# Two pre-norm transformer layers with a routed mixture of experts: gate weights that travel with the routed row, normalisation moved to ScalarE, and one step of a DMA queue reordered

## The chip, the cores and the metric

One core of a Trainium2 chip. The metric is device time in microseconds of one execution of the whole program; the runs of the kernel before are three.

## The reference, cut to what matters

The input is 8 sequences of 1024 tokens, 256 wide, float32. Four sub-layers follow, each with a residual and a layer norm in front: windowed attention with projection, a mixture of experts, block-sparse attention, a ternary linear layer. The change touches the parts around the mixture of experts:

```
logits = xf @ gate_w.T                       # 8 experts
topk_logits, topk_idx = top_k(logits, 2)
topk_w = softmax(topk_logits)                # = 0.5 +- 0.5*tanh((l1 - l2)/2)
for e in range(8):
    y = (silu(xf @ wg[e].T) * (xf @ wu[e].T)) @ w_down[e].T      # 384 hidden
    out = out + comb[:, e:e+1] * y
x = x + out + shared(xf)                     # one shared expert for every token
x = x + attention(layernorm(x))              # starts with q, k, v projections
```

## The kernel before, in words

The kernel is a row of stages with a barrier between two; each names its tiles with a prefix. Every engine has its program written out in order, and waits on semaphores; nothing is scheduled by a planner. The tokens stay in SBUF as `x_res`, 64 tiles of 128 tokens. A chunk is 4 tiles (512 tokens), 16 chunks in all. Products are done in three float16 terms from high and low parts (`split3`, lines 83 to 85).

`stage_project` (prefix `p`, runs twice: `p0` before the first attention, `p1` before the second). For each chunk: statistics of the rows (`bn_stats`, `bn_aggr`, VectorE lines 329, 332), square root on ScalarE (`root`, 407), reciprocal and normalisation on VectorE (`norm`, 337 and 343, four instructions of 128x256), transposes on TensorE (451), high part on ScalarE (`high`, 414), low part on VectorE (`low`, 352), 48 matmuls for q, k and v, then ScalarE writes q and k twice (`queries_keys`, 422 and 426, eight instructions), GpSimd subtracts to get their low parts (397), VectorE writes v (`values`, 361). Loads and stores are on SyncE's queue. In `p1` the statistics are preceded by merging: the two routed results of a token are loaded from DRAM (`yb`) and VectorE adds each with its gate weight to `x_res` (323, eight instructions of 128x256 a chunk).

`stage_route` (prefix `g`), a loop over the 16 chunks `s`. ScalarE normalises the rows of chunk `s+2` and writes their high part into `xrow` (`row_hi`, 1274 and 1280), VectorE writes the low part (`row_lo`, 1323), SyncE turns the rows with four DMA transposes (`turn`, 1197) into `xt`, TensorE makes the gate logits (`gates`), VectorE finds the top two (`top2`, 1330 to 1354) and the row number of each token in its experts' lists (`slots`, 1359 to 1368), GpSimd sends the rows there by indirect DMA into the DRAM table `xs` (1242, eight a chunk). Beside that the shared expert is computed in two halves of a chunk (`up`, `down` on TensorE; `silu` and `high` on ScalarE; `hidden`, part of the low parts and `add_y` on VectorE; `low` on GpSimd, 1250). And the weights of all experts, 27 parts, are brought in through a buffer of two (`w32`): SyncE loads (`load`, 1183), ScalarE makes the high part (`weight_hi`, 1267), VectorE the low part (`weight_lo`, 1318). Three parts come ahead of the loop, two in each of chunks 0 to 11 (`weight_parts`). The order of SyncE's queue in a chunk is: turn chunk `s+2` (waits until `row_lo` has written it), load the two weight parts, store a finished chunk of `x_res`. ScalarE's order in a chunk is: first half of the shared expert, `row_hi(s+2)`, first weight part, second half, second weight part. A difference of the two top logits per token is kept, and at the end of the stage one Tanh (1312) and two VectorE instructions (1450, 1451) make the gate weights.

`stage_routed` (prefix `e`): 71 tiles `j` of 256 rows of `xs`, each of one expert. SyncE transposes the rows in and loads two words of each row, token and expert (`col`, 1602); VectorE works out from them where each result goes (`address`, 1675 to 1685, five small instructions); TensorE does the expert's products (54 matmuls), ScalarE empties the result with one plain copy (`copy_y`, 1657, 128x512), GpSimd scatters the rows to `y2` (1630). At tile 4 four DMAs bring the gate weights into the order of tiles that the second layer uses (`swap_halves`).

Of the kernel before, what the change touches and what calls it, by code (L numbers as in the profile page):

```python
# [219 lines left out]
def stage_project(nc, tag, x_res, ident, w_in, b_in, qx, kx, vx, x_dram=None, y2=None, gate_w=None):  # L220
# [3 lines left out]
    with ExitStack() as ctx:  # L224
# [11 lines left out]
        std, rstd = sb("std", [P, 2, TC], F32), sb("rstd", [P, 2, TC], F32)  # L236
# [12 lines left out]
        rooted, inverted, normed = sem("rooted"), sem("inverted"), sem("normed")  # L249
# [8 lines left out]
        def _(sp):  # L258
# [52 lines left out]
        def _(dve):  # L311
            due = [0] * NC

            def statistics(c):
                k, r = c % 2, c % YR if merging else c
                due[r] += 16 * ((6 if c % 2 == 0 else 2) if merging else 1)
                dve.wait_ge(loaded[r], ONE + due[r])
                for n in range(2 if merging else 0):
                    if n:
                        dve.wait_ge(merged, ONE + 2 * TC * c + TC)  # L320
                    for t in range(TC):
                        ti = c * TC + t
                        dve.scalar_tensor_tensor(out=x_res[:, ti, :], in0=yb[:, r, n, t, :],
                                                 scalar=gate_w[:, ti, n:n + 1], in1=x_res[:, ti, :],
                                                 op0=ALU.mult, op1=ALU.add).then_inc(merged, 1)
                if merging:
                    dve.wait_ge(merged, ONE + 2 * TC * (c + 1))
# [41 lines left out]
            norm(0)  # L369
# [7 lines left out]
            norm(1)  # L377
            statistics(2)
            dve.wait_ge(s_set, ONE + 2)
            for c in range(NC):  # L380
                if c + 1 < NC:
                    low(c + 1)
                if c + 2 < NC:
                    norm(c + 2)
# [16 lines left out]
        def _(act):  # L401
# [6 lines left out]

            def high(c):
# [6 lines left out]
            def queries_keys(c):  # L416
# [3 lines left out]
                for m in range(4):  # L420
                    act.wait_ge(qk_ready, ONE + 4 * c + m + 1)
# [9 lines left out]
            root(1)  # L431
            act.wait_ge(s_w, ONE + 64)
            for j in range(3):
                act.activation(wh[:, j], w32[:, j], ACT.Copy, scale=WS).then_inc(s_wh, 1)
            high(0)
# [631 lines left out]
def swap_halves(eng, dst, src, sem):  # L1067


    d, s = (a.rearrange("p (b t) w -> p b t w", t=TB) for a in (dst, src))  # L1070
    eng.dma_start(d[0:64, :, 0, :], s[0:64, :, 0, :]).then_inc(sem, 16)
    eng.dma_start(d[64:P, :, 0, :], s[64:P, :, TB - 1, :]).then_inc(sem, 16)
    eng.dma_start(d[0:64, :, 1:TB, :], s[64:P, :, 0:TB - 1, :]).then_inc(sem, 16)
    eng.dma_start(d[64:P, :, 1:TB, :], s[0:64, :, 1:TB, :]).then_inc(sem, 16)


# [17 lines left out]
class Routing:  # L1094


    def __init__(self, sb, w_turned):
# [4 lines left out]
        self.w, self.w_turned = sb("moe_w", [P, NT, 2], F32), w_turned  # L1102


def stage_route(nc, tag, x_res, mean, rstd, ident, gate_in, up_in, down_in, ew, rt, xs, x_dram):


    with ExitStack() as ctx:
        def sb(n, shape, dt):
# [12 lines left out]
        xrow = sb("xrow", [P, XR, TC, 2 * D + 4], F16)  # L1122
# [8 lines left out]
        dif, th = sb("dif", [P, NT], F32), sb("th", [P, NT], F32)  # L1131
# [10 lines left out]
        zeros = spare[:, 1500:1500 + 2 * (D + 2)].rearrange("p (t w) -> p t w", t=2)  # L1142
# [23 lines left out]
        x_stored, counted, dif_done, th_done, table, pads, padded = (sem(n) for n in (  # L1166
            "x_stored", "counted", "dif_done", "th_done", "table", "pads", "padded"))
# [9 lines left out]
        def _(sp):  # L1177
# [45 lines left out]
        def _(pool):  # L1223
# [40 lines left out]
        def _(act):  # L1264
# [16 lines left out]

            def silu(s, h, f):
# [28 lines left out]
            act.wait_ge(dif_done, ONE + 1)  # L1311
            act.activation(th[:, :], dif[:, :], ACT.Tanh, scale=0.5).then_inc(th_done, 1)

        @block.vector
        def _(dve):
# [11 lines left out]
            def top2(c):  # L1327
# [3 lines left out]
                dve.wait_ge(routed, b + 1)  # L1331
                for t in range(TC):
# [631 lines left out]
```

## Time and profile before

| | us |
|---|---|
| median of three runs | 3210.08 (3198.16 to 3218.04) |
| the profiled execution | 3220.43 |
| its span, first to last instruction | 3218.7 |
| mean granted TensorE clock, share of full | 0.832 |

The profiled execution is one run with the hardware profiler; its rows say what each engine did and when, in us from the start of the span. A row of the timeline gives start, duration, engine, line, operation, output<-inputs, count, and in brackets the engine's idle time before it with what ended it; "x4" is four such instructions in a row, with their duration together. Stages by time: `p0` from 9 to 170, `g` from 1175 to 1545, `e` from 1549 to 1988, `p1` from 1996 to 2208; attention and the rest fill what lies between and after.

### The profile page before, as it was taken

The page shows a single profiled execution, that of the slowest core. Times are in us where ns is not written, and L with a number is a line of the kernel's source. Part 1 is how long each engine was busy: PE and PEld are TensorE (multiplying, and loading weights), DVE is VectorE, ACT ScalarE, POOL GpSimd, SP SyncE. Part 2 cuts the span into 40 slices and gives each one's busy share as a digit, 9 for nine tenths or more (in the row PEclk, how much of TensorE's full clock was granted, in tenths as well). Part 3 has the DMA queues.
Part 4 walks back from the last instruction along what each step waited for, and adds up shares of the span by engine and source line. Part 5 has one row for each costly group of instructions (what it writes and reads, how often), then busy time and mean ns, then how long its engine had stood idle before and what let it go on. Part 6 is the DMA issues. An engine that isn't in the chain of part 4 may idle for free. (4 is left out here: it accounts for less than half of the span.)

```text
span 3218.7 us, 81517 instructions
## 1 busy us (share of the span) xinstructions
PE 2391.7 (74%) x25933; PEld 1381.7 (43%) x25933; DVE 2043.7 (63%) x5809; ACT 1565.5 (49%) x3598; POOL 984.4 (31%) x1271
## 2 busy tenths in 40 slices
PE   7917888888856645668799996783588888888336
PEld 4602222222215534556688885441133333333225
DVE  7827777777715544445444443991789888887278
ACT  5605666666650023334244442551278777778202
POOL 3503433434434014556466664341000000000005
PEclk9957877878876667778899998896699999999658
DMA  6521222222201114444555344563022222221123
GB/s 205 201 87 32 63 64 68 64 62 69 68 29 55 42 49 118 115 122 138 118 130 145 90 90 101 189 230 113 21 68 65 62 65 62 63 67 46 52 72 104
DMA packets 361817, 290.14 MB, mean 90 GB/s; under 512 B 226304, under 2 KB 294656, under 8 KB 361408
## 3 DMA queue, kind: packets, MB, share of 16 engines
q1 hardware_dynamic: 348448, 249.32, 27.2%
q0 software_dynamic: 12960, 35.54, 3.4%
q8 instruction: 235, 3.85, 0.5%
q14 instruction: 174, 1.43, 0.1%
HBM read 133.46 MB, written 123.62 MB: 80 GB/s over the span
## 5 line engine op out<-in xcount | busy, mean ns | idle before, releaser
L766 ACT ACTIVATE a_pr<-a_pst 128x384 f32<-128x384 f32 (+3 forms) x2176 | 935.9, 483 | 398.7 <-PE a_pst L790 360.7
L714 DVE TENSOR_REDUCE a_mx<-a_psc 128x1 f32<-128x384 f32 (+2 forms) x1152 | 592.2, 567 | 140.1 <-PE a_psc L790 130.3
L709 DVE CUSTOM_DVE_ANT_0 a_cut<-a_psc,row_mask 128x384 bf16<-128x384 f32 (+1 forms) x1024 | 499.7, 522 | 209.1 <-PE a_psc L790 174.6
L857 PE MATMUL a_po<-a_pr,a_ve 128*17 128x128 f32 (+3 forms) x10496 | 622.8, 328 | 1.6 <-ACT a_pr L766 1.0
L790 PE MATMUL a_psc<-a_ke,a_qe 52*128 52x128 f16 (+5 forms) x3072 | 411.8, 312 | 249.5 <-DMA a_ke<-mrow 114.5
L790 PE MATMUL a_pst<-a_qe,a_ke 53*128 53x128 f16 (+5 forms) x3072 | 399.4, 303 | 104.4 <-ACT a_pr L766 44.3
L688 POOL TENSOR_SCALAR_AFFINE_SELECT a_pr<-a_pr 128x512 f32<-128x512 f32 x448 | 275.0, 634 | 496.2 <-ACT a_pr L766 496.2
L1796 POOL TENSOR_TENSOR x_res<-x_res,t_bias 128x256 f32 (+1 forms) x64 | 44.5, 726 | 967.4 <-DVE t_xn L185 967.4
L790 PEld LDWEIGHTS a_pst<-a_qe,a_ke 53*128 53x128 f16 (+1 forms) x3072 | 122.6, 95 | 468.3 <-ACT a_pr L766 234.3
L790 PEld LDWEIGHTS a_psc<-a_ke,a_qe 52*128 52x128 f16 (+1 forms) x3072 | 130.0, 97 | 407.1 <-issue 160.2
L857 PEld LDWEIGHTS a_po<-a_pr,a_ve 128*17 128x17 f32 x10496 | 198.3, 98 | 239.0 <-issue 154.8
L1691 DVE SCALAR_TENSOR_TENSOR e_hid<-e_pgu,e_gate 128x256 f32<-128x256 f32 x213 | 90.4, 425 | 247.1 <-ACT e_gate L1646 247.1
L83 PE MATMUL e_pgu<-e_xt,uh 128*128 128x256 f16 x852 | 233.5, 274 | 14.2 <-DMA e_xt<-xs 14.2
L84 PE MATMUL e_pgu<-e_xt,uh 128*128 128x256 f16 x852 | 233.5, 274 | 0.0
L85 PE MATMUL e_pgu<-e_xt,ul 128*128 128x256 f16 x852 | 233.4, 274 | 0.0
L397 POOL TENSOR_TENSOR p_stg<-p_qk,p_stg 128x512 f16<-128x512 f32 x128 | 148.8, 1176 | 223.8 <-ACT p_qk L426 222.1
L1646 ACT ACTIVATE e_gate<-e_pgu 128x256 f32<-128x256 f32 x213 | 81.0, 381 | 244.7 <-PE e_pgu L85 244.7
L83 PE MATMUL g_pgu<-g_xt,uh 128*128 128x256 f16 x384 | 118.8, 309 | 103.6 <-DVE g_hid L1375 103.6
L957 PE MATMUL c_ptok<-ident,c_ot 68*128 68x68 f32 x512 | 73.0, 307 | 153.9 <-DMA c_ot<-ox 110.8
L1622 POOL TENSOR_TENSOR e_hl<-e_hid,e_hh 128x256 f16<-128x256 f32 x213 | 141.2, 675 | 130.6 <-ACT e_hh L1650 129.1
L1242 POOL DMA_INDIRECT xs<-g_xrow,g_slot x128 | 126.8, 991 | 83.6 <-DVE g_slot L1368 51.3
L1630 POOL DMA_INDIRECT y<-e_yst,e_dest x142 | 138.1, 973 | 37.0 <-issue 34.4
(217 smaller groups left out, 4324.0 us busy)
## 6 DMA issues: line engine op xcount, KB each, us to landing
a_qe<-qx SPq DMA_DIRECT2D x384, 64.0 KB, 2.6
a_ke<-kx SPq DMA_DIRECT2D x384, 64.0 KB, 2.6
vx<-p_vst SPq DMA_DIRECT2D x32, 544.0 KB, 3.1
a_ve<-vx SPq DMA_DIRECT2D x64, 272.0 KB, 3.2
ox<-a_ost SPq DMA_DIRECT2D x256, 68.0 KB
c_ot<-ox SPq DMA_DIRECT2D x32, 544.0 KB
qx<-p_stg SPq DMA_DIRECT2D x64, 256.0 KB, 3.3
kx<-p_stg SPq DMA_DIRECT2D x64, 256.0 KB, 3.1
```

The source lines that it names most:

```text
L83: pe.matmul(out, stat_hi(p), mov_hi(p), start=(a == 0), stop=False)
L84: pe.matmul(out, stat_hi(p), mov_lo(p), start=False, stop=False)
L85: last = pe.matmul(out, stat_lo(p), mov_hi(p), start=False, stop=(a == n - 1))
L397: pool.tensor_tensor(stg[:, b % 2, m, 1, cols], qk32[:, m, :], stg[:, b % 2, m, 0, cols], ALU.subtract).then_inc(qk_lo, 1)
L688: pool.affine_select(out=edge, in_=edge, compare_op=ALU.is_ge, fill=0.0, base=0, pattern=[[0, 4], [sign, width]], channel_multiplier=-sign)\
L709: dve.tensor_tensor_reduce(out=cut[:, n % 4, 0:width], in0=psc[n % RING][:, 0:width], in1=row_mask[:, at:at + width], scale=1.0, scalar=-3 ...
L714: dve.tensor_reduce(out.unsqueeze(1), psc[n % RING][:, 0:width], AXX, ALU.max)\
L766: act.activation(pr[s % SLOTS][:, h // 2, h % 2, 0:width], pst[k % RING][:, 0:width], ACT.Exp, scale=scale).then_inc(p_ready, 1)
L790: last = pe.matmul(outs[par][:, col:col + count], stats[par], movs[par](tok, count), start=(k == 0), stop=(k == len(pieces) - 1), skip_gro ...
L857: last = pe.matmul(po[h][32 * a:32 * a + VW, tok % CH:tok % CH + w], ve[g][:, t, a * VW:(a + 1) * VW], pr[s % SLOTS][:, a // 2, a % 2, col ...
L1622: pool.tensor_tensor(hl[:, j % 2, f, :], hid[:, f, :], hh[:, j % 2, f, :], ALU.subtract)\
L1630: pool.indirect_dma_start(y2[:, :], bass.IndirectOffsetOnAxis(ap=dest[:, g, t:t + 1], axis=0), yst[:, g, t, :], None).then_inc(scattered[g ...
```

## The change

It does five things. (1) In `stage_project`, the normalisation of a row goes from VectorE to ScalarE: VectorE computes reciprocal and `shift` = -mean*reciprocal (`invert`), ScalarE applies both in four instructions, put between the second and third output of `queries_keys`. (2) The merge in `p1` becomes two plain additions of 128x1024. (3) In `stage_route`, SyncE loads the weight parts of a chunk ahead of turning chunk `s+2`, and ahead of the loop it loads part 2 before turning chunk 0. (4) The Tanh of a chunk's logit difference is taken in that chunk (`weigh`), written into the row, which grows from 516 to 518 float16 values and is sent as 32-bit words. (5) In `stage_routed`, `address` has three more small instructions that turn that value into the gate weight of the row (`share`), `copy_y` is two instructions of 128x256 with that weight as scale and waits for `address`; `swap_halves` and the gate weights at the end of `stage_route` go.

```diff
@@ stage_project, SyncE and VectorE
-                    sp.wait_ge(merged, ONE + 2 * TC * (c - YR + 1))
+                    sp.wait_ge(merged, ONE + 2 * (c - YR + 1))
...
-                        dve.wait_ge(merged, ONE + 2 * TC * c + TC)
-                    for t in range(TC):
-                        ti = c * TC + t
-                        dve.scalar_tensor_tensor(out=x_res[:, ti, :], in0=yb[:, r, n, t, :],
-                                                 scalar=gate_w[:, ti, n:n + 1], in1=x_res[:, ti, :],
-                                                 op0=ALU.mult, op1=ALU.add).then_inc(merged, 1)
+                        dve.wait_ge(merged, ONE + 2 * c + 1)
+                    dve.tensor_tensor(xc, xc, yb[:, r, n, :, :], ALU.add).then_inc(merged, 1)
...
-            def norm(c):
+            def invert(c):
                 k = c % 2
                 dve.wait_ge(rooted, ONE + c + 1)
+                if c >= 2:
+                    dve.wait_ge(normed, ONE + TC * (c - 1))
                 dve.reciprocal(rstd[:, k, :], std[:, k, :]).then_inc(inverted, 1)
                 dve.wait_ge(inverted, ONE + c + 1)
                 dve.wait_ge(gathered, ONE + TC * (c + 1))
-                if c >= 2:
-                    dve.wait_ge(turned, ONE + EC * (c - 1))
-                for t in range(TC):
-                    dve.tensor_scalar(xn[:, k, t, :], x_res[:, c * TC + t, :], mv[:, k, t, 0:1], rstd[:, k, t:t + 1],
-                                      ALU.subtract, ALU.mult).then_inc(normed, 1)
+                dve.scalar_tensor_tensor(out=shift[:, k, :], in0=mv[:, k, :, 0], scalar=-1.0, in1=rstd[:, k, :],
+                                         op0=ALU.mult, op1=ALU.mult).then_inc(shifted, 1)
@@ stage_project, ScalarE
+            def norm(c):
+                k = c % 2
+                if c >= 2:
+                    act.wait_ge(turned, ONE + EC * (c - 1))
+                act.wait_ge(shifted, ONE + c + 1)
+                for t in range(TC):
+                    act.activation(xn[:, k, t, :], x_res[:, c * TC + t, :], ACT.Identity, bias=shift[:, k, t:t + 1],
+                                   scale=rstd[:, k, t:t + 1]).then_inc(normed, 1)
...
                 for m in range(4):
+                    if m == 2 and c + 2 < NC:
+                        norm(c + 2)
@@ stage_route, SyncE
+            load(2)
             turn(0)
-            load(2)
             turn(1)
             for s in range(NC + 2):
+                for n in weight_parts(s):
+                    load(n)
                 if s + 2 < NC:
                     turn(s + 2)
-                for n in weight_parts(s):
-                    load(n)
@@ stage_route, GpSimd
-                            xs[:, :], bass.IndirectOffsetOnAxis(ap=slot[:, c * TC + t, n:n + 1], axis=0),
-                            xrow[:, c % XR, t, :], None).then_inc(scattered[c % XR], 16)
+                            xs[:, :].bitcast(U32), bass.IndirectOffsetOnAxis(ap=slot[:, c * TC + t, n:n + 1], axis=0),
+                            xrow[:, c % XR, t, :].bitcast(U32), None).then_inc(scattered[c % XR], 16)
...
+                pool.wait_ge(weighed, ONE + s + 1)
@@ stage_route, ScalarE
+            def weigh(c):
+                act.wait_ge(routed, ONE + c * RT + 10)
+                act.activation(xrow[:, c % XR, :, 2 * D + 4:2 * D + 6].bitcast(F32), dif[:, c % 2, :].unsqueeze(2),
+                               ACT.Tanh, scale=0.5).then_inc(weighed, 1)
...
+            weigh(0)
             for s in range(NC):
                 for h in range(2):
                     silu(s, h, 0)
                     silu(s, h, 1)
+                    if h and s + 1 < NC:
+                        weigh(s + 1)
                     high(s, h, 0)
...
-            act.wait_ge(dif_done, ONE + 1)
-            act.activation(th[:, :], dif[:, :], ACT.Tanh, scale=0.5).then_inc(th_done, 1)
@@ stage_routed
                 sp.dma_start(col[:, j % GR, :, :],
-                             xs[bass.ds(row, SL), 2 * D:2 * D + 4].bitcast(U32).rearrange("(t p) w -> p t w", p=P))\
+                             xs[bass.ds(row, SL), 2 * D:2 * D + 6].bitcast(U32).rearrange("(t p) w -> p t w", p=P))\
...
-                if j == GR:
-                    swap_halves(sp, rt.w_turned[:, :, :], rt.w[:, :, :], w_moved)
...
-                act.activation(yst[:, g, :, :], py[j % 2][:, :, :], ACT.Copy).then_inc(y_copied, 1)
+                act.wait_ge(addressed, ONE + AD * (j + 1))
+                for t in range(2):
+                    act.activation(yst[:, g, t, :], py[j % 2][:, t, :], ACT.Copy, scale=share[:, j % 2, t:t + 1])\
+                       .then_inc(y_copied, 1)
...
+                dve.tensor_scalar(sign[:, k, :], second[:, k, :], -YS / T, 0.5 * YS, ALU.mult, ALU.add)\
+                   .then_inc(addressed, 1)
...
+                dve.tensor_tensor(part[:, k, :], sign[:, k, :], col[:, g, :, 2].bitcast(F32), ALU.mult)\
+                   .then_inc(addressed, 1)
+                dve.wait_ge(addressed, b + 7)
+                if j >= 2:
+                    dve.wait_ge(y_copied, ONE + 2 * (j - 1))
+                dve.tensor_scalar(share[:, k, :], part[:, k, :], 0.5 * YS, None, ALU.add).then_inc(addressed, 1)
```

## Rows read from the trace of the kernel before

**Rows 1.** Stretches: busy us of PE, PEld, DVE, ACT, POOL, then clock, DMA share, GB/s.

```profile
40.00:160.00 120.00, 120.00 (x775) 76.84 (x774) 105.90 (x214) 82.78 (x151) 65.17 (x56) 1.00 0.51 188
1190.00:1486.00 296.00, 187.88 (x1712) 154.81 (x1713) 131.33 (x486) 109.44 (x238) 147.60 (x147) 0.79 0.43 116
1486.00:1525.00 39.00, 37.43 (x382) 32.32 (x381) 26.91 (x107) 17.46 (x44) 32.19 (x36) 1.00 0.52 158
1600.00:1900.00 300.00, 300.00 (x2750) 268.21 (x2748) 129.25 (x408) 129.78 (x356) 200.73 (x255) 1.00 0.51 119
2031.00:2181.00 150.00, 123.99 (x729) 74.83 (x728) 148.17 (x325) 78.34 (x143) 60.26 (x53) 0.94 0.62 210
```

**Rows 2.** Waits of stage g, 1175 to 1545: total us, times, longest.

```profile
ACT uh L1267 <- DMA g_w<-up_w: 90.0, 8, 12.7
...
ACT dh L1267 <- DMA g_w<-down_w: 49.1, 5, 11.8
```

**Rows 3.** Timeline of SyncE's queue in stage g.

```profile
1179.75 5.26 SPq L1197 DMA_TRANSPOSE g_xt<-g_xrow  x4
...
1345.08 5.25 SPq L1197 DMA_TRANSPOSE g_xt<-g_xrow  x4
1350.37 1.08 SPq L1183 DMA_DIRECT2D g_w<-up_w  x2
```

**Rows 4.** Timeline of ScalarE in stage g.

```profile
1202.57 1.06 ACT L1280 ACTIVATE g_xrow<-g_xn 128x1024 f16<-128x1024 f32 x1
...
1354.98 0.84 ACT L1267 ACTIVATE uh<-g_w 128x768 f16<-128x768 f32 x1 [11.19 <-DMA g_w<-up_w]
...
1484.55 2.06 ACT L1274 ACTIVATE g_xn<-x_res,g_shift,rstd 128x256 f32<-128x256 f32 x4
1486.72 1.06 ACT L1280 ACTIVATE g_xrow<-g_xn 128x1024 f16<-128x1024 f32 x1
...
1500.35 1.06 ACT L1280 ACTIVATE g_xrow<-g_xn 128x1024 f16<-128x1024 f32 x1
```

**Rows 5.** Timeline of VectorE in stage g.

```profile
1190.28 0.18 DVE L1330 TENSOR_SCALAR g_logit<-g_small 128x32 f32<-128x32 f32 x1
...
1343.82 1.22 DVE L1323 SCALAR_TENSOR_TENSOR g_xrow<-g_xn,g_xrow 128x1024 f16<-128x1024 f32 x1 [1.47 <-ACT g_xrow L1280]
...
1479.85 0.99 DVE L1318 SCALAR_TENSOR_TENSOR dl<-g_w,dh 128x768 f16<-128x768 f32 x1 [0.35 <-ACT dh L1267]
...
1487.81 1.64 DVE L1323 SCALAR_TENSOR_TENSOR g_xrow<-g_xn,g_xrow 128x1024 f16<-128x1024 f32 x1 [1.47 <-ACT g_xrow L1280]
```

**Rows 6.** Timeline of GpSimd in two chunks without weights.

```profile
1496.59 0.99 POOL L1242 DMA_INDIRECT xs<-g_xrow,g_slot  x1 [0.31 <-DVE g_slot L1368]
...
1510.31 0.98 POOL L1242 DMA_INDIRECT xs<-g_xrow,g_slot  x1 [0.31 <-DVE g_slot L1368]
```

**Rows 7.** Timeline of VectorE through one chunk of p1.

```profile
2107.87 3.90 DVE L343 TENSOR_SCALAR p_xn<-x_res,p_mv,p_rstd 128x256 f32<-128x256 f32 x4
2111.69 1.27 DVE L361 SCALAR_TENSOR_TENSOR p_vst<-p_pv,p_bv 128x512 f32<-128x512 f32 x2
2112.89 3.36 DVE L323 SCALAR_TENSOR_TENSOR x_res<-p_yb,moe_wt,x_res 128x256 f32<-128x256 f32 x8
...
2118.03 1.26 DVE L352 SCALAR_TENSOR_TENSOR p_xl<-p_pt,p_xh 128x512 f16<-128x512 f32 x2
...
2119.40 3.97 DVE L343 TENSOR_SCALAR p_xn<-x_res,p_mv,p_rstd 128x256 f32<-128x256 f32 x4
```

**Rows 8.** Single lines: duration ns, minimum/median/maximum, first and last start.

```profile
L343 DVE TENSOR_SCALAR p_xn<-x_res,p_mv,p_rstd x128: 402/1240/1320, 16.5 to 2179.9; 128x256 f32<-128x256 f32 x128
...
L1058 DVE TENSOR_TENSOR x_res<-x_res,c_att x16: 1206/1215/1217, 3036.6 to 3126.5; 128x1024 f32 x14, 128x1024 f32<-128x1024 f32 x2
```

**Rows 9.** Tanh after Silu, and the one table load for Silu.

```profile
L1312 ACT ACTIVATE g_th<-g_dif x1: 238/238/238, 1539.1 to 1539.1; 128x64 f32<-128x64 f32 x1
...
L1285 ACT ACT_TABLE_LOAD x1 | 1.3, 1283 | 0.0
```

More of the change, by code:

```diff
@@ L217, in split_ready, with stage_project @@
             eng.wait_ge(self.lo_done[e], ONE + c + 1)
[L220 removed]
+def stage_project(nc, tag, x_res, ident, w_in, b_in, qx, kx, vx, x_dram=None, y2=None):
     merging = y2 is not None
@@ L235, in stage_project @@
         st, mv = sb("st", [P, 2, TC, 6], F32), sb("mv", [P, 2, TC, 2], F32)
-        std, rstd = sb("std", [P, 2, TC], F32), sb("rstd", [P, 2, TC], F32)
+        std, rstd, shift = (sb(n, [P, 2, TC], F32) for n in ("std", "rstd", "shift"))
         xn = sb("xn", [P, 2, TC, D], F32)
@@ L315, in statistics @@
                 k, r = c % 2, c % YR if merging else c
+                xc = x_res[:, c * TC:(c + 1) * TC, :]
                 due[r] += 16 * ((6 if c % 2 == 0 else 2) if merging else 1)
@@ L368, in _ @@
             statistics(1)
-            norm(0)
+            invert(0)
+            invert(1)
             dve.wait_ge(s_w, ONE + 64)
@@ L376, in _ @@
             low(0)
-            norm(1)
             statistics(2)
@@ L383, in _ @@
                 if c + 2 < NC:
-                    norm(c + 2)
+                    invert(c + 2)
                 values(c)
@@ L431, in _ @@
             root(1)
+            norm(0)
             act.wait_ge(s_w, ONE + 64)
@@ L434, in _ @@
                 act.activation(wh[:, j], w32[:, j], ACT.Copy, scale=WS).then_inc(s_wh, 1)
+            norm(1)
             high(0)
@@ L1064, in _ @@
             stats.finish(dve)
[L1067 to L1074, printed above, removed]
 class ExpertWeights:
@@ L1094, with __init__ @@
 class Routing:
-    def __init__(self, sb, w_turned):
+    def __init__(self, sb):
         self.expert, self.row = sb("tab_expert", [P, NJ], U32), sb("tab_row", [P, NJ], U32)
@@ L1121, in stage_route @@
         xn = sb("xn", [P, TC, D], F32)
-        xrow = sb("xrow", [P, XR, TC, 2 * D + 4], F16)
+        xrow = sb("xrow", [P, XR, TC, 2 * D + 6], F16)
         xt = sb("xt", [P, XR, 2 * EC, CH], F16)
@@ L1130, in stage_route @@
         slotf, slot = sb("slotf", [P, 2, TC, 2], F32), sb("slot", [P, NT, 2], U32)
-        dif, th = sb("dif", [P, NT], F32), sb("th", [P, NT], F32)
+        dif = sb("dif", [P, 2, TC], F32)
         gate, hid = sb("gate", [P, FC, SL], F32), sb("hid", [P, FC, SL], F32)
@@ L1141, in stage_route @@
         gone = [spare[:, 256 + n * NJ * E:256 + (n + 1) * NJ * E].rearrange("p (j e) -> p j e", e=E) for n in range(2)]
-        zeros = spare[:, 1500:1500 + 2 * (D + 2)].rearrange("p (t w) -> p t w", t=2)
+        zeros = spare[:, 1500:1500 + 2 * (D + 3)].rearrange("p (t w) -> p t w", t=2)
         tj = [sb(f"tj{n}", [P, NJ], F32) for n in range(6)]
@@ L1165, in stage_route @@
         y_ready, y_added = [sem(f"y_ready{h}") for h in range(2)], [sem(f"y_added{h}") for h in range(2)]
-        x_stored, counted, dif_done, th_done, table, pads, padded = (sem(n) for n in (
-            "x_stored", "counted", "dif_done", "th_done", "table", "pads", "padded"))
+        x_stored, counted, weighed, table, pads, padded = (sem(n) for n in (
+            "x_stored", "counted", "weighed", "table", "pads", "padded"))
         RT = 21
@@ L1331, in top2 @@
                 dve.wait_ge(routed, b + 1)
+                if c >= 2:
+                    dve.wait_ge(weighed, ONE + c - 1)
                 for t in range(TC):
@@ L1446, in table_of_tiles @@
                    .then_inc(table, 1)
-            def gate_weights():
-                dve.wait_ge(th_done, ONE + 1)
-                dve.tensor_scalar(rt.w[:, :, 0], th[:, :], 0.5 * YS, 0.5 * YS, ALU.mult, ALU.add).then_inc(table, 1)
-                dve.tensor_scalar(rt.w[:, :, 1], th[:, :], -0.5 * YS, 0.5 * YS, ALU.mult, ALU.add).then_inc(table, 1)
-                dve.wait_ge(table, ONE + 26)
             dve.scalar_tensor_tensor(out=shift[:, :], in0=mean[:, :], scalar=-1.0, in1=rstd[:, :],
@@ L1483, in _ @@
                 add_y(s, 0)
-                if s + 2 == NC:
-                    dve.wait_ge(routed, ONE + (s + 1) * RT + 17)
-                    dve.sem_inc(dif_done, 1)
             add_y(NC - 1, 1)
-            gate_weights()
+            dve.wait_ge(table, ONE + 24)
         @block.tensor
@@ L1567, in stage_routed @@
         xt = sb("xt", [P, GX, 2 * EC, SL], F16)
-        col = sb("col", [P, GR, 2, 2], U32)
+        col = sb("col", [P, GR, 2, 3], U32)
         gate, hid = sb("gate", [P, FC, SL], F32), sb("hid", [P, FC, SL], F32)
@@ L1575, in stage_routed @@
         dest = sb("dest", [P, GR, 2], U32)
+        sign, part, share = (sb(n, [P, 2, 2], F32) for n in ("sign", "part", "share"))
         pgu = [ctx.enter_context(nc.psum_tensor(f"{tag}_pgu{f}", [P, 2, SL], F32)) for f in range(FC)]
@@ L1587, in stage_routed @@
         scattered = [sem.from_zero(f"scattered{g}") for g in range(GR)]
-        w_moved, x_loaded = sem("w_moved"), sem("x_loaded")
-        AD = 5
+        x_loaded = sem("x_loaded")
+        AD = 8
         sem.start()
@@ L1626, in scatter @@
                 g = j % GR
-                pool.wait_ge(y_copied, ONE + j + 1)
+                pool.wait_ge(y_copied, ONE + 2 * (j + 1))
                 pool.wait_ge(addressed, ONE + AD * (j + 1))
@@ L1674, in address @@
                 dve.wait_ge(loaded[g], ONE + 16 * (j // GR + 1))
-                dve.tensor_copy(colf[:, k, :, :], col[:, g, :, :]).then_inc(addressed, 1)
+                dve.tensor_copy(colf[:, k, :, :], col[:, g, :, 0:2]).then_inc(addressed, 1)
                 dve.wait_ge(addressed, b + 1)
@@ L1720, in down @@
                 if j >= 2:
-                    pe.wait_ge(y_copied, ONE + j - 1)
+                    pe.wait_ge(y_copied, ONE + 2 * (j - 1))
                 for f in range(FC):
```

17 lines of the change are left out of this document (7 added, 10 removed).

## The prediction

> **What bounds the kernel now.** I read the table of stretches first, since the change touches three stages with different limits [rows 1]. In `p0` (40 to 160) TensorE is busy 120.00 of 120 us at full clock: 775 matmuls, 56 to a chunk, so 8.67 us a chunk, and nothing on another engine shows. In `e` (1600 to 1900) it is 300.00 of 300 us. In `p1` (2031 to 2181) VectorE has 148.17 of 150 us and TensorE waits. In `g` (1190 to 1486) no engine is full: TensorE 188, GpSimd 148 of 296 us, clock 0.79. Such a stretch is waiting for something outside the engines, and the list of waits says what: ScalarE waited 90.0 + 49.1 us in 13 pieces for weight parts to land [rows 2]. The timeline shows why. `turn` of the next chunk is ahead of the loads on SyncE's queue; its four transposes take 5.25 us to issue, from 1345.08, the loads follow at 1350.37, and ScalarE gets the first at 1354.98 after 11.19 us idle [rows 3, 4]. ScalarE is in order, so the second half of the shared expert stands behind that wait. The second part of `row_hi` starts at 1202.57 in turn 0 of the loop and at 1486.72 in turn 12, 23.7 us a turn; from turn 12 to 13, which have no weights, the step is 13.63 us [rows 4].
>
> **Part 3, the loads ahead of `turn`.** The loads of a chunk now stand before a wait on `row_lo(s+2)` and behind one on the buffer, which the previous chunk's `weight_lo` frees. After that VectorE still does a low part, `add_y`, `slots` and three products, and ScalarE a `row_hi` of 2.06 + 1.06 us, before the part is wanted. I put that at 8 us after the first buffer is free, from the order of the program and the chunk of 13.63 us. A load took 1354.98 - 1350.37 = 4.6 us behind four transposes. So it is hidden with about 3 us to spare, and the 11 us stall goes. `turn` is pushed back only by the issue of two loads, 1.08 us, and its rows are wanted a chunk later.
>
> What is late next is what bounds a chunk without weights. GpSimd repeats there in 1510.31 - 1496.59 = 13.72 us with 0.31 us idle at that point, waiting for `slots` [rows 6]. A second ring has the same length: `row_hi`, `row_lo`, `top2`, `hidden`, `slots`, `hidden`, `high`, `row_hi`, 13.63 us between ScalarE and VectorE [rows 4]. Two `weight_lo` of 0.93 to 0.99 us lie on that ring, with 0.35 us for the second `weight_hi` [rows 5], less about 0.5 us of waiting that they fill: 13.63 + 1.75 = 15.4 us, and 0.1 for the chunk's Tanh and contention, 15.5. Bounds: 14.0 if the ring absorbs most of it, 17.5 if the loads land later in a denser queue. Twelve periods go from (1486.72 - 1202.57)/12 = 23.7 us to 15.5: 98 us, bounds 74 and 116. The DMA share, 0.43 at 23.7 us a chunk, becomes 0.66 at 15.5.
>
> Ahead of the loop the order costs. `turn(0)` started at 1179.75 and now waits for load 2, which waits for the first `weight_lo`; that puts it near 1185.7. But the first `top2` began only at 1190.28, behind the third `weight_lo` [rows 3, 5], so not all 6 us reach it. I take 3, bounds 0 and 6.
>
> **Part 4.** `weigh` is one instruction of 128x4 per chunk, under the 238 ns of the 128x64 one [rows 9], and its input is ready before the `hidden` that ScalarE waits for anyway. GpSimd's new wait on it was met a chunk ahead. The Tanh before came after Silu with no table load of its own; the stage has the one load of 1283 ns [rows 9]. I take no switch inside the loop, and at most one more load ahead of it, beside TensorE's first products. The one Tanh and two small instructions at the end save under 0.5 us.
> The Trainium skill ("ScalarE: Activation LUTs", section Table sets: the hidden batching unit) says that functions of different sets cost a load at each change and should be batched by set; interleaving Tanh with Silu would then speak against this change. Taken so, it is the third rival below; the trace agrees that both are served by one set here.
>
> **Part 1 and 2, `p1`.** The four `norm` instructions took 3.90 us of an 11.53 us chunk [rows 7]. One such takes 402 ns at its shortest and 1240 in the median [rows 8]: it is slow when GpSimd's subtraction runs. It goes, against a reciprocal (as now) and a `shift` of 0.2 us. Merging took 3.36 us for eight; two additions of 1215 ns take 2.45 [rows 7, 8]. VectorE falls to 11.53 - 3.9 - 0.9 + 0.2 = 6.9 us a chunk, and TensorE's 8.67 would be next. ScalarE is busy 82.78 us over 13.84 chunks in `p0`, 5.98 each, and gets 2.06 more [rows 1, 4]: 8.0, still under 8.67. But a chain is longer: from the end of v's products, `values` (0.8 after it), merging 2.45, statistics 1.7, root and start 0.3, two pairs of outputs (four of the ten large instructions in ScalarE's 5.98 us, 0.57 each: 2.3), `norm` 2.06, and 0.1 of hand-overs give 9.6 us until the next transposes may start. Each chunk's rows are normalised two ahead, so two periods hold this chain and one TensorE chunk: (9.6 + 8.67)/2 = 9.1 us. GpSimd's subtractions now run while VectorE merges. In `g` an instruction with two SBUF inputs took 1.22 us, and 1.64 where it started beside a GpSimd subtraction [rows 5]; so I take 9.4, bounds 8.67 and 10.5. Over 13 chunks: 13 x (11.53 - 9.4) = 28 us, bounds 13 and 37.
> The Trainium skill ("SBUF — State Buffer", section SBUF: two separate sides) has the port pair of VectorE and GpSimd as an exclusive lock, also taken by a VectorE instruction with two SBUF inputs when GpSimd reads SBUF. By it the second addition would wait for one subtraction of 1.1 us (60.26 us over 53), and the chunk would be (9.6 + 1.1 + 8.67)/2 = 9.7 us, 24 us saved; the 1.64 beside 1.22 points the same way.
>
> `p0` has nothing to gain, being TensorE's. ScalarE's 8.0 us fits, and `norm` is done before the transposes need it. At its start and at that of `p1`, `norm(0)` and `norm(1)` stand with the weight parts on ScalarE, 2 us each, but the transposes of chunk 1 also wait for the low part of chunk 0: I take 0 in `p0` and -1 in `p1`, which merges faster, bounds -3 and +4 together.
>
> **Part 5, `e`.** TensorE is full, 5.9 us a tile (2750 matmuls in 300 us, 54 each) [rows 1]. ScalarE has 2.5 us a tile and gets under 0.3, VectorE 2.5 and at most 1.5, GpSimd the same work. The new wait of `copy_y` on `address` has the next tile's silus behind it on ScalarE; `address(j-1)` stands before `hidden(j)` on VectorE, so it is done when ScalarE comes to it. I take 0, bounds -1 and +5 (cover gone in a few tiles). The scatter of 32-bit words moves the same rows.
>
> **Sum.** -98 + 3 - 28 - 1 + 0 = -124 us. The profiled execution, 3220.4, would be 3096. It lies 10 us over the median of the runs, so against that median I say 3210 - 124 = 3086.
>
> **Rivals.**
> 1. The stall goes, but TensorE becomes the bound because its clock stays where it is. For: the clock of this stretch is 0.79 [rows 1], and a chunk needs about 13.1 us at full clock (37.43 of 39 us, at 13.7 us a chunk). Against: in 1486 to 1525 it is 1.00, with work not much denser than I expect. 13.1/0.79 = 16.6 us a chunk, 85 us saved in place of 98: 3099.
> 2. ScalarE bounds the projections. For: 8.0 us of work in 8.67 leaves 0.67 for its waits, and it now waits for statistics, for `shift` and for transposes in one order. Against: the norms stand where its inputs are old. If the waits take twice the spare time, `p0` loses 0.7 x 14 = 10 us: 3096.
> 3. Each Tanh switches tables twice: 32 loads of 1283 ns on the ring of ScalarE and VectorE, 41 us: 3127. Against: [rows 9].
> 4. Slower: the row pitch of `xs`, from 1032 to 1036 bytes, makes the transposing loads of `e` slow. They share a DMA load of 0.51 with the rest, 3.0 of 5.9 us a tile [rows 1]. To cost the 124 us that the rest gives, a tile must reach 7.65 us, so DMA work would have to grow 2.6 times, and from that point the whole is slower; at 3 times it is 9.0 us a tile, 71 x 3.1 = 220 us: 3306. Against: 1032 is no round pitch either.
>
> **How the numbers follow.** Forecast 0.73, first rival 0.12, second 0.07, third 0.05, fourth 0.02, the rest 0.01 for no change. The likeliest gives 3086. The best ends together (-116, -37, 0) give 3057, less the spread of the runs, 3050; the worst (-74 + 6 - 13) give 3129, which takes in rivals 1 to 3. About 1% (32 us) is what a measurement can tell from no change, with runs 20 us apart: faster 0.96, same 0.02, slower 0.02.
>
> **What would show it.** In the new profile of `g`: no wait of ScalarE for `g_w` over 2 us after the first, `row_hi` about every 15.5 us in chunks 1 to 12, clock near 1.00, the stage about 95 us shorter. In `p1`: transposes every 9.4 us, VectorE no longer full. In `p0` 8.67 us a chunk, in `e` 5.9 us a tile, and one table load in `g`, two at most. Wrong it would be if weights still stall ScalarE, if a tile of `e` grows, or if ACT_TABLE_LOAD appears per chunk.

## The result and the profile after

The changed kernel takes 3103.28 us (median of 4 runs, 3093.11 to 3108.87), the kernel before beside it 3214.06 (3198.16 to 3219.72): a ratio of 0.966, 95% interval 0.962 to 0.970. That is 111 us less, where 124 were forecast. The profiled execution took 3108.87 us, with a span of 3107.1, against 3220.43 and 3218.7.

Where the time went is read best from the stages. Each begins at the first instruction that only it has, in the two profiled executions:

| stage | before, us | after, us | difference | forecast |
|---|---|---|---|---|
| `p0` to the first scores | 216.6 | 216.3 | -0.3 | -1 with `p1`'s start |
| `a0`, `c0` (unchanged) | 958.4 | 958.1 | -0.3 | 0 |
| `g` | 385.2 | 292.6 | -92.6 | -95 |
| `e` | 435.9 | 433.0 | -2.9 | 0 |
| `p1` to the first scores | 265.1 | 250.5 | -14.6 | -28 |
| `a1`, `c1` and the rest (unchanged) | 957.5 | 956.6 | -0.9 | 0 |

The unchanged part agrees here by chance. Over the fourteen profiles of this study `a0`, `c0`, `a1` and `c1` together lie between 1828 and 1861 us, with no edit in them, while `g` comes within 1 to 3 us again in every kernel with the same `g`. So the stages below are compared by their own length, and totals that lie less than 15 us apart are not told apart. Two rows of the table need the same care. The changed `e` takes 433.0 to 433.8 us in most profiles and 436.2 to 436.3 in three (e3, e4, e6), the old one 435.5 and 435.9, so its -2.9 is no gain that is shown. The changed `p1` takes 248.2 to 248.8 us in the three other profiles with the same `p1` (e2, e8, e9), so the gain there is 14.6 to 17 us.

The table of stretches after, with a stretch of `p0`, `g`, `e` and `p1` in turn; busy us of PE, PEld, DVE, ACT and POOL, then granted clock, DMA share and GB/s:

```profile
40.00:160.00 120.00, 120.00 (x775) 76.87 (x774) 57.96 (x174) 106.59 (x203) 64.47 (x57) 1.00 0.51 188
1210.00:1400.00 190.00, 158.35 (x1652) 136.25 (x1653) 139.67 (x459) 104.84 (x242) 149.31 (x143) 0.99 0.63 174
1500.00:1800.00 300.00, 300.00 (x2750) 268.40 (x2748) 146.53 (x560) 147.61 (x407) 200.29 (x255) 1.00 0.50 120
1935.00:2070.00 135.00, 121.00 (x746) 74.70 (x743) 102.75 (x210) 102.12 (x195) 64.08 (x52) 0.96 0.71 233
```

Against [rows 1]: `p0` and `e` are TensorE's as before, to the matmul. In `g` the clock has gone from 0.79 to 0.99 and TensorE is busy 83% of the stretch, not 64%. In `p1` VectorE is no longer full (76%), and yet TensorE is not full either.

The waits of ScalarE in `g` after, against [rows 2]:

```profile
ACT g_hh L1294 <- DVE g_hid L1382: 74.0, 62, 8.9
ACT g_xrow L1283 <- DVE g_dif L1344: 29.3, 15, 4.1
...
ACT dh L1266 <- DMA g_w<-down_w: 3.8, 1, 3.8
```

139 us of waiting for weight parts have become 3.8, once, ahead of the loop. What is left is waiting for VectorE: 103.3 us in these two rows, where the same view of the kernel before has 30.4. It has grown, but by less than the wait that went.

ScalarE's timeline in `g`, against [rows 4]:

```profile
1187.54 0.84 ACT L1266 ACTIVATE dh<-g_w 128x768 f16<-128x768 f32 x1 [3.77 <-DMA g_w<-down_w]
1188.40 1.28 ACT L1283 ACT_TABLE_LOAD   x1
1193.75 0.21 ACT L1283 ACTIVATE g_xrow<-g_dif 128x4 f32<-128x4 f32 x1 [4.06 <-DVE g_dif L1344]
1193.97 1.28 ACT L1289 ACT_TABLE_LOAD   x1
...
1233.11 2.06 ACT L1273 ACTIVATE g_xn<-x_res,g_shift,rstd 128x256 f32<-128x256 f32 x4
1248.92 2.06 ACT L1273 ACTIVATE g_xn<-x_res,g_shift,rstd 128x256 f32<-128x256 f32 x4
...
1375.40 2.06 ACT L1273 ACTIVATE g_xn<-x_res,g_shift,rstd 128x256 f32<-128x256 f32 x4
```

`row_hi` comes every 15.8 us (1233.11 to 1375.40 in nine steps; 15.5 forecast, 23.7 before). The first Tanh and the first Silu load a table each, and no other load follows in the loop.

### The profile page after: what moved, and what is told of

Read it like the earlier page. It is cut to its first block and busy times, and to the rows that moved or that the text cites. A ratio compares the mean times of both kernels' runs of the same rounds, so it can differ in the third digit from the quotient of the medians.

```text
span 3107.1 us, 81888 instructions
## 1 busy us (share of the span) xinstructions
PE 2357.4 (76%) x25933; PEld 1358.1 (44%) x25933; DVE 1970.9 (63%) x5828; ACT 1649.8 (53%) x3813; POOL 991.8 (32%) x1271
## 5 line engine op out<-in xcount | busy, mean ns | idle before, releaser
L966 PEld LDWEIGHTS c_ptok<-ident,c_ot 68*128 68x128 f32 x512 | 57.8, 197 | 166.9 <-issue 82.5
```

## The experiments

Each kernel ran beside the kernel before, and the ratio is to that. "A chunk of p1" is the mean of the steps between the transposes of one chunk and the next, from the third chunk on (11.55 us before, 10.3 in the changed kernel). Where a count of matmuls is given, it is the time by that count (56 a chunk) in the stretch 1935 to 2070; a few records are missing from some traces, so it can come out up to 0.2 us off.

**e1: the order of the queue alone.** In the kernel before:

```diff
             for s in range(NC + 2):
+                for n in weight_parts(s):
+                    load(n)
                 if s + 2 < NC:
                     turn(s + 2)
-                for n in weight_parts(s):
-                    load(n)
```

> The kernel before with one edit of the change alone: in the loop of g's SyncE queue the weight loads stand ahead of turn. Nothing else is taken over, and the prologue is as before. Theory: the order of the queue is the whole gain of g, which the two traces put at 385.2 - 292.6 = 92.6 us; so 90 to 97 us off the kernel before, a row_hi every 15.5 to 15.8 us in place of 23.7, ScalarE's waits for weight parts gone, p0, p1 and e as before. Rival: the order alone leaves a wait that another part of the change removes (the one Tanh at the end, or the prologue's load), and less than 80 us come.

Measured: ratio 0.971 (0.967 to 0.976), 86 us; `g` 290.1 us, 95.1 less than before; `p1` 265.4 and `e` 435.5, as before. `row_hi` every 15.83 us, and of the waits for weight parts this is left:

```profile
ACT dh L1267 <- DMA g_w<-down_w: 4.0, 1, 4.0
```

The order of two statements is the whole gain of `g`. It is even 2.5 us shorter than the changed kernel's, which also has `load(2)` ahead of `turn(0)`: from the stage's first instruction to the loop's first `row_hi` it is 25.4 us before and 25.3 here and in e2, and 28.6 in the changed kernel. That is the "+3" of the forecast. The totals are 86 us apart and `g` 95, which the spread of the unchanged stages covers: in the profile of e1 they were 26 us longer.

**e2: the change without that order.** In the changed kernel the loop's loads stand behind `turn` again, and `load(2)` behind `turn(0)`.

> The changed kernel with the old order of g's SyncE queue, in the loop and ahead of it; all else of the change stays. Theory: g goes back to 385 us and a row_hi every 23.7 us, the time to 92 us above the changed kernel; what is left against the kernel before is p1's 15 us and e's 3, so 0.992 to 0.995 of it. Rival: the parts help each other, and it is more than 100 us above the changed kernel.

Measured: ratio 0.996 (0.993 to 0.999), 11 us less than before; `g` 387.3 us, and the old waits are back:

```profile
ACT uh L1266 <- DMA g_w<-up_w: 92.6, 8, 13.3
ACT dh L1266 <- DMA g_w<-down_w: 50.5, 5, 12.5
```

The parts add up: `g` is 2 us longer than before, within what it varies by, and the gain is `p1`'s (248.3 us here). The ratio lies just above the 0.992 to 0.995 that I expected. The weighing by Tanh in `g` costs nothing that shows.

**e3: `p1` without GpSimd's subtraction.** In the changed kernel (with the low part of the staging tile filled with zero once):

```diff
-                    pool.tensor_tensor(stg[:, b % 2, m, 1, cols], qk32[:, m, :], stg[:, b % 2, m, 0, cols],
-                                       ALU.subtract).then_inc(qk_lo, 1)
+                    w = 8 if merging else CH
+                    part = slice(cols.start, cols.start + w)
+                    pool.tensor_tensor(stg[:, b % 2, m, 1, part], qk32[:, m, 0:w], stg[:, b % 2, m, 0, part],
+                                       ALU.subtract).then_inc(qk_lo, 1)
```

> The changed kernel, but in p1 GpSimd's subtraction for the low parts of queries and keys covers 8 of 512 columns; the other columns are filled with zero once, so the low parts are left out. Theory: the subtractions beside VectorE's additions made these slow (1318 ns in the median, up to 2170, where 1200 was taken), and the chain from v's products to the next transposes by it longer than 9.6 us. Without them the additions take 1.2 us each and a chunk of p1 (9.6 + 8.67)/2 = 9.1 us in place of 10.3: 15 us less than the changed kernel. Rival: the chain is long for another reason (ScalarE's order, the hand-overs), and p1 stays at 10.0 to 10.3 us a chunk.

Measured: a chunk 9.23 us by the count (819 matmuls in 135 us) and 9.3 by the steps, where 9.1 was expected; `p1` 237.5 us, 13 less than in the changed kernel. The total, ratio 0.964 (0.960 to 0.968), doesn't show it: the unchanged stages were 19 us longer in that profile. The additions, first in the changed kernel, then here (busy us, mean ns of one):

```profile
L322 DVE TENSOR_TENSOR x_res<-x_res,p_yb 128x1024 f32<-128x1024 f32 x26 | 43.1, 1656 | 0.4
```

```profile
L322 DVE TENSOR_TENSOR x_res<-x_res,p_yb 128x1024 f32<-128x1024 f32 x26 | 31.7, 1220 | 0.4
```

1656 ns beside the subtractions, 1220 without: 3.3 us a chunk against 2.44. The theory holds, in the size too.

**e4: statistics ahead of the copies of v.** In the changed kernel:

```diff
-                values(c)
                 if c + 3 < NC:
                     statistics(c + 3)
+                values(c)
```

> The changed kernel, but in both projections VectorE does the statistics (and merging) of a chunk ahead of the copies of v, not behind them; the same instructions. Theory: the chain of p1 begins at the end of v's products only because the copies stand ahead of the merging. With it parted, VectorE's 6.9 to 8 us of work a chunk fit in TensorE's 8.67, and p1 goes from 10.3 to 8.7 - 9.1 us a chunk: 16 to 21 us less than the changed kernel. p0 stays. Rival: a chain that goes through ScalarE (outputs of queries and keys, norm) or VectorE's contended work is as long, and p1 stays at 9.8 or more.

Measured: `p1` 241.7 us, 9 less where 16 to 21 were expected, a chunk 9.8 us. It is neither the one nor the other. The chain is parted, and a new wait has come. ScalarE's outputs and the additions no longer show; VectorE waits for the rows of y:

```profile
DVE x_res L322 <- DMA p_yb<-y: 21.5, 4, 6.1
```

SyncE's queue and VectorE say why:

```profile
1966.58 2.96 SPq L288 DMA_DIRECT2D qx<-p_stg  x4
1969.58 3.00 SPq L288 DMA_DIRECT2D kx<-p_stg  x4
1972.62 1.30 SPq L270 DMA_DIRECT2D p_yb<-y  x1
...
1981.78 2.48 DVE L322 TENSOR_TENSOR x_res<-x_res,p_yb 128x1024 f32<-128x1024 f32 x2 [5.99 <-DMA p_yb<-y]
```

The loads are behind eight stores, which take 6 us to issue. Their buffer had been free for three chunks. The total, ratio 0.968 (0.963 to 0.972), can't be told from the changed kernel's.

**e5: plain additions, norm back on VectorE.** The changed kernel with `norm` and `invert` of the projections as they were before.

> The changed kernel with norm of both projections back on VectorE as before; merging stays two plain additions. VectorE is then the bound of p1 again. Theory: eight instructions of 3.36 us become two of 2.45, so a chunk of p1 goes from 11.5 (before) to 10.6 us. Rival: beside GpSimd's subtractions two long additions lose as much as they save (they took 2.6 to 4.0 us in the changed kernel), and a chunk stays at 11.2 or more. g and e as in the changed kernel; the whole 5 to 15 us above it.

**e6: norm on ScalarE, merging in eight as before.**

```diff
-                    dve.tensor_tensor(xc, xc, yb[:, r, n, :, :], ALU.add).then_inc(merged, 1)
+                    for t in range(TC):
+                        ti = c * TC + t
+                        dve.scalar_tensor_tensor(out=x_res[:, ti, :], in0=yb[:, r, n, t, :], scalar=one[:, 0:1],
+                                                 in1=x_res[:, ti, :], op0=ALU.mult, op1=ALU.add).then_inc(merged, 1)
```

> The changed kernel with the merging of p1 as before, eight scalar_tensor_tensor (with a scalar of one, since the rows are already weighted); norm stays on ScalarE. Theory: the chain from v's products through merging to the next transposes is 0.9 us longer than in the changed kernel, a chunk 10.3 + 0.45 = 10.7 us or a little more; the move of norm is then worth 0.8 us a chunk of the 1.25 that p1 gained. Rival: the eight short instructions fit better between GpSimd's subtractions, and a chunk is 10.3 or less, so that the plain additions brought nothing.

Measured: e5 has `p1` at 252.5 us (ratio 0.970, 0.966 to 0.973), e6 at 266.4 (ratio 0.971, 0.968 to 0.974); before it was 265.1 and after 250.5. So the plain additions bring 12.6 us alone, and the move of `norm` alone brings nothing; on top of the additions it brings another 2 to 4 us. Merging of e5, then of e6:

```profile
L322 DVE TENSOR_TENSOR x_res<-x_res,p_yb 128x1024 f32<-128x1024 f32 x26 | 31.6, 1217 | 0.5
```

```profile
L324 DVE SCALAR_TENSOR_TENSOR x_res<-p_yb,p_one,x_res 128x256 f32<-128x256 f32 x96 | 64.8, 736 | 0.4
```

By busy time a chunk, merging takes 2.43 us in e5 and 5.4 in e6 (64.8 in 12 chunks); before it took 3.33 (43.3 us in 13 chunks of the stretch 2031 to 2181), and in the changed kernel 3.3. `norm` on VectorE had stood in GpSimd's way (four instructions of 1.04 us where the shortest is 0.40 [rows 8]). Moved to ScalarE, it left its place to the merging, which then stood in it. My expectation for e5 was met (10.67 for 10.6 us a chunk, by steps of 10.63 to 10.70). That for e6 was too low: 11.5 for 10.7, since I had the chain longer by 0.9 us and it was longer by 5.4 - 3.3 = 2.1; the clock in its stretch was 0.90 besides, where the changed kernel has 0.96.

**e7: rows of y asked for two chunks earlier.** In e4:

```diff
-                if c + ahead < NC:
-                    load_y(c + ahead)
+                for n in range(c + ahead + (2 if c else 0), c + ahead + 3):
+                    if merging and n < NC:
+                        load_y(n)
```

> As e4_statistics_early, but on SyncE's queue of p1 the rows of chunk c + 6 are asked for where chunk c + 4 was, ahead of the stores of chunk c (the same four buffers). In e4 VectorE waited 21.5 us in four pieces for these rows, once per pair of chunks, behind the stores of queries and keys. Theory: the place in the queue is the cause; the waits go, and a chunk of p1 takes TensorE's 8.7 to 8.9 us in place of 9.6 to 9.7: 12 us less than e4. Rival: the DMA engines themselves are the bound (share 0.74), the waits come back elsewhere, and a chunk stays above 9.3.

**e12: the same loads in the changed kernel,** with the statistics left in their place.

> The changed kernel with only the rows of y asked for two chunks earlier in p1, and the statistics behind the copies of v as before. Theory: in the changed kernel VectorE did not wait for these rows (the chain from v's products was later than they), so the stage stays at 10.0 to 10.3 us a chunk, 250 us in all; the place of the statistics is what opens the gain, and the loads are the wait that follows. Rival: earlier loads alone shorten p1 by over 5 us.

Measured: e7 has `p1` at 227.2 us, 23 less than the changed kernel, and the transposes are 8.67 us apart, which is TensorE's own time. VectorE no longer waits for rows of y; these are the longest waits of VectorE and ScalarE in the stretch 1935 to 2040:

```profile
DVE p_xl L349 <- ACT p_xh L420: 6.0, 12, 0.5
ACT p_stg L430 <- PE p_pqk L85: 5.2, 12, 0.5
DVE p_vst L358 <- PE p_pv L85: 3.0, 12, 0.3
```

The additions are as slow as ever there (1658 ns), but nothing waits for them. In e12 `p1` stays at 248.8 us, as expected. Both edits are needed, in that order: the chain hid the late rows. The totals, 0.966 (0.962 to 0.969) and 0.966 (0.960 to 0.972), are covered by the spread of the attention stages.

**e8: slots early in `g`.** In the changed kernel:

```diff
             for s in range(NC):
-                slots(s)
...
                 hidden(s, 1)
+                if s + 1 < NC:
+                    slots(s + 1)
                 for n in weight_parts(s):
                     weight_lo(n)
```

(and `slots(0)` ahead of the loop).

> The changed kernel, but in g VectorE does slots(s + 1) right after hidden(s, 1), ahead of the two weight_lo, low and add_y, where it stood behind them. In the changed kernel GpSimd waits there up to 1.2 us a chunk; its own work is 8 scatters at 1.27 us and four subtractions of 1.1, 14.7 us. Theory: GpSimd is the bound of g now, a chunk goes from 15.8 to 14.7 us, and g from 292.6 to 280. Rival: the ring between ScalarE and VectorE with weight_lo on it is the bound, and the chunk stays at 15.6 or more.

Measured: ratio 0.963 (0.960 to 0.965); `g` 274.6 us, 18 less than the changed kernel, a chunk 14.34 where 14.7 was expected. The instructions are the same. `slots` now ends 3 us after the products that it waits for begin (`ranks`, on TensorE; 1293.4 and 1290.4), where it ended 6 us after (1294.4 and 1288.3). But GpSimd, which it releases, waits for it hardly less (0.8 us a chunk, 1.2 before). What has changed is how long GpSimd's subtractions take. The changed kernel, then e8, each from 1220 to 1380:

```profile
L1248 POOL TENSOR_TENSOR g_hl<-g_hid,g_hh 128x256 f16<-128x256 f32 x42 | 47.1, 1142 | 0.5
```

```profile
L1248 POOL TENSOR_TENSOR g_hl<-g_hid,g_hh 128x256 f16<-128x256 f32 x46 | 31.8, 710 | 4.0 <-ACT g_hh L1294 2.6
```

Four a chunk, each 0.43 us shorter, are 1.7 us; the chunk lost 1.47. In the changed kernel one pair runs from 1291.39 to 1293.58, beside VectorE's `weight_lo` and `low`; in e8 a pair runs from 1291.68 to 1292.98, beside a `hidden` that reads PSUM and the small instructions of `slots`. And TensorE waited for these low parts in the changed kernel (total us, times, longest, in the same stretch); in e8 it has no such wait:

```profile
PE g_py L83 <- POOL g_hl L1248: 26.8, 20, 1.6
```

So the order of VectorE's program made GpSimd's chunk shorter. Whether the shorter subtractions alone give the 1.47 us, or the earlier release as well, was not tried apart.

**e9 to e11.** The changed kernel again, then with the edits of e7 and e8 together, then with one more of GpSimd's subtractions on VectorE:

> The changed kernel once more, unaltered, beside the two below, as their measure: a ratio of 0.963 to 0.969 to the kernel before, p1 at 10.1 to 10.3 us a chunk and g at 292 us. What its unchanged attention stages differ by from the first profile (a0 755.9, a1 769.0 us) is the size of what no edit causes; by the runs so far, up to 15 us either way.

> The changed kernel with the three edits that shortened a stage: statistics ahead of the copies of v and rows of y asked for two chunks earlier (p1), slots right after the second half's products (g). Theory: they touch different stages and add up: p1 23 us and g 18 us less than the changed kernel, so 3062 to 3070 us where that has 3105, ratio 0.951 to 0.955. Rival: the shorter stages leave TensorE's clock lower in the attention stages that follow, or their spread eats it, and less than 25 us come.

> As e10_all_three, and in g VectorE does the low part of the second third of the hidden units too, which GpSimd had. GpSimd's chunk falls from about 14 to 12.5 us (two subtractions of 0.7 to 1.1 us fewer), VectorE's rises from 11.0 to 12 - 12.8. Theory: with slots early, GpSimd is the bound of g (14.34 us a chunk in e8), so a chunk goes to 13.3 - 13.7 us, TensorE's 13.1 at full clock being next, and g loses 8 to 12 us more. Rival: the ring between ScalarE and VectorE is as long as GpSimd's work, the subtractions lie on it, and g stays or grows.

| | median, us | ratio (interval) | `g` | `p1` | unchanged four |
|---|---|---|---|---|---|
| e9 | 3122.27 | 0.965 (0.960 to 0.969) | 295.2 | 248.5 | 1849.3 |
| e10 | 3079.77 | 0.952 (0.948 to 0.957) | 275.2 | 227.3 | 1844.0 |
| e11 | 3092.10 | 0.956 (0.953 to 0.960) | 277.5 | 227.8 | 1841.0 |

e10 is 42 us faster than the changed kernel in the same series, which is 20 in `g` and 21 in `p1`: the gains add up, and it beats both kernels. e11 misses: a chunk of `g` was expected at 13.3 to 13.7 us. GpSimd's subtractions of e11 and what it waited for:

```profile
L1249 POOL TENSOR_TENSOR g_hl<-g_hid,g_hh 128x256 f16<-128x256 f32 x22 | 16.5, 751 | 13.8 <-ACT g_hh L1295 13.6
```

Its work fell from 126.85 us (e8) to 111.29 in 160, and `row_hi` still came every 14.24 us. So GpSimd's work was not the bound of `g` after e8. TensorE is busy 147 of these 160 us; what holds the chunk at 14.2 to 14.3 us stays open.

## Why the prediction was right, and where it was off

**Part 3.** Right in mechanism and in size. The stall came from the order of the queue and went with it (e1, e2). The period was forecast at 15.5 and is 15.8 us, the start at +3 and is +3.2 (28.6 against 25.4). What holds a chunk once the stall is gone was named less well. The forecast had two rings of one length, GpSimd's with its wait for `slots` and one between ScalarE and VectorE, and laid the two `weight_lo` on the second only. In the changed kernel GpSimd stood idle for `slots` only 1.2 us of 15.8 and TensorE waited for it 26.8 us in 160 (the rows at e8), so GpSimd was probably on the path too, with subtractions that were longer beside `weight_lo`. The 15.5 is near 15.8, but these runs do not show that the ring which the forecast took is the one that sets it. The first rival falls: the clock rose to 0.99, in e1 too, where nothing but the order was changed.

**Part 4.** Two table loads ahead of the loop and none in it: the third rival falls. The Trainium skill ("ScalarE: Activation LUTs", section Table sets: the hidden batching unit) asks for batching only across sets. Here Tanh following Silu needs no load, while Silu following the first Tanh did: the order of the first two decides.

**Part 1 and 2.** Here the forecast was off: 28 us, and 14.6 came (up to 17 in the other profiles), within the bounds of 13 to 37 but near the lower one. Two terms of the step failed. (The chain's terms also add up to 9.7 us and not to 9.6, which is 0.05 us a chunk.) The first is the merging. The step had "two additions of 1215 ns", raised the chunk from 9.1 to 9.4 for contention, and so priced the merging at about 3.0 (a chain of 2 x 9.4 - 8.67 = 10.1 us). The pair of rows that this rested on, 1.22 us and 1.64 beside a subtraction [rows 5], does not part the two cases: the one of 1.22, at 1343.82, ran beside subtractions as well (a pair from 1343.21 to 1345.57). It is longer where it counts. One chain of the changed kernel, from v's products to the late transposes:

```profile
1997.29 0.69 DVE L357 SCALAR_TENSOR_TENSOR p_vst<-p_pv,p_bv 128x512 f32<-128x512 f32 x1 [0.55 <-PE p_pv L85]
1997.90 4.03 DVE L322 TENSOR_TENSOR x_res<-x_res,p_yb 128x1024 f32<-128x1024 f32 x2
2001.97 1.41 DVE L326 BATCH_NORM_STATS2 p_st<-x_res 128x6 f32<-128x256 f32 x4
2003.40 0.38 DVE L329 BATCH_NORM_AGGREGATE p_mv<-p_st 128x2 f32<-128x6 f32 x4
...
2003.82 0.30 ACT L403 ACTIVATE p_std<-p_mv,p_eps 128x4 f32<-128x4 f32 x1 [4.17 <-DVE p_mv L329]
2004.03 0.67 ACT L429 ACTIVATE p_stg<-p_pqk,p_bqk_s 128x512 f16<-128x512 f32 x1
...
2006.30 2.07 ACT L411 ACTIVATE p_xn<-x_res,p_shift,p_rstd 128x256 f32<-128x256 f32 x4
...
1997.60 3.25 POOL L393 TENSOR_TENSOR p_stg<-p_qk,p_stg 128x512 f16<-128x512 f32 x2 [1.91 <-ACT p_qk L433]
...
2008.43 1.09 PE L460 MATMUL p_pt<-ident,p_xn 128*128 128x128 f32 x8 [2.50 <-ACT p_xn L411]
```

The pieces are those of the forecast, in its order, and each has its size but one: two additions and two subtractions begin together and take 4.03 and 3.25 us, where they take 2.43 and 2.3 apart. From 1997.29 to 2008.43 are 11.1 us, against 9.6 forecast, and the additions have all of the difference (1.6 us). The other late chain, with additions of 3.28 us from 2019.65, is 10.4 us (2019.05 to 2029.43). The rule of the Trainium skill that I had weighed ("SBUF — State Buffer", section SBUF: two separate sides), an exclusive port pair, gave 9.7 us a chunk; the trace agrees in direction, with both engines' instructions longer, and the measured 10.3 is nearer to it than to my 9.4. e3, which removes the subtractions, is at 9.23, and the formula without contention gives 9.1.

The second is TensorE's clock. The formula put TensorE's chunk at 8.67 us after each late one. The transposes of the changed kernel:

```profile
1947.29 1.09 PE L460 MATMUL p_pt<-ident,p_xn 128*128 128x128 f32 x8 [1.75 <-ACT p_xn L411]
1956.02 1.04 PE L460 MATMUL p_pt<-ident,p_xn 128*128 128x128 f32 x8
1967.36 1.09 PE L460 MATMUL p_pt<-ident,p_xn 128*128 128x128 f32 x8 [2.50 <-ACT p_xn L411]
1977.78 1.04 PE L460 MATMUL p_pt<-ident,p_xn 128*128 128x128 f32 x8
1988.36 1.09 PE L460 MATMUL p_pt<-ident,p_xn 128*128 128x128 f32 x8 [1.75 <-ACT p_xn L411]
```

Four chunks are 8.73, 11.34, 10.42 and 10.58 us, 41.1 together or 10.3 each, and the pattern repeats. After a wait of 1.75 us the next chunk takes 8.73; after one of 2.50 it takes 10.42. The clock by stretches in such a chunk:

```profile
2008.00:2010.00 2.00, 1.57 (x11) 1.16 (x12) 1.96 (x2) 2.00 (x5) 0.39 (x1) 0.89 0.98 316
2010.00:2012.00 2.00, 2.00 (x6) 0.73 (x5) 1.94 (x9) 1.77 (x5) 2.00 (x2) 0.50 0.06 19
2012.00:2014.00 2.00, 2.00 (x8) 0.79 (x7) 1.26 (x4) 1.50 (x4) 0.65 (x2) 0.75 0.50 188
2014.00:2016.00 2.00, 2.00 (x11) 0.88 (x9) 0.00 (x0) 2.00 (x5) 1.45 (x2) 1.00 1.01 380
```

It fell to the lower level, 1.2 GHz, for a good 3 us after the wait of 2.50 us, and half of that time is the 1.7 us that the chunk took more. With that chunk at 8.73 us, as after the shorter wait, the mean would be 9.85. So the clock has 0.4 of the 0.9 us a chunk that the forecast missed; that share is read from the trace and was not tried by itself. It follows from the first: in e3, without the subtractions, TensorE's waits are 0.94 us and its clock is 1.00 in the same stretch.

What the forecast had not seen at all is what e5 and e6 show: relieving VectorE of `norm` was priced as 3.9 us a chunk off the engine that bounds, and is worth nothing alone and 2 to 4 us in all beside the additions. The engine was relieved (102.75 of 135 us, which is 7.8 a chunk where 6.9 was forecast), but the bound was already a chain through the copies of v, the merging and ScalarE, just as long. The forecast named this chain and took it for shorter than it was.

**Part 5, the rivals.** A tile of `e` is 5.9 us as before and TensorE full; the wider rows cost nothing, and the fourth rival falls. `p0` kept 8.67 us a chunk with ScalarE busy 106.59 of 120 us, 7.7 a chunk: the second rival falls, if narrowly.

## What to carry to other kernels

Read a queue that issues both prefetches and work with a wait in the order of what is wanted first: two statements changed places here for 95 of 111 us. When work is moved off a full engine, look for the chain that comes next and for what will then run at the same time on the engine that slows it; here the price of contention went to the instruction that took the place (e6), and to GpSimd's side too (e8). When an engine in order has a task that needs nothing new (statistics) behind one that waits (copies), exchange them, and then look for the transfer that the old wait had hidden.

## What the runs showed of the hardware

An elementwise instruction of VectorE with both inputs in SBUF grows by a third beside GpSimd's (1220 to 1656 ns in the mean at 128x1024), and eight short ones grow more than two long ones (0.42 to 0.68 us each, by busy time; 1.22 to 1.66). GpSimd's grow too: its subtraction of 128x256 took 0.71 us in the mean in e8 and 1.14 in the changed kernel, by what VectorE did at the same time. An activation of ScalarE (128x256) beside the same work kept its 0.60 us, with the subtractions and without. Each of TensorE's waits of 2.50 us in the `p1` of the changed kernel was followed by a chunk of 10.4 us with the clock at its lower level in part of it (10.2 to 10.3 in e9), and each of 1.75 us by a chunk of 8.73.
